# Exponentials of the routing on GpSimd instead of ScalarE, in twelve of sixteen row groups

## The chip, the cores and the metric

The kernel runs on one NeuronCore of a Trainium2 chip. TensorE (PE) multiplies matrices, VectorE (DVE) does elementwise work and reductions, ScalarE (ACT) evaluates functions, GpSimd (POOL) runs elementwise work in software and issues indirect DMAs, SyncE (SP) issues DMAs. Each engine takes its instructions in the order of the program and waits at semaphores. The metric is the device time of the launch in microseconds (us).

## The reference

```python
x = hidden_states                                  # (4, 2048, 256) fp32
x = x + _layernorm(attention(_layernorm(x)))       # "bump" attention, 16 heads
x = x + _layernorm(ffn(_layernorm(x)))
# attention, per head: out_i = sum_j max(0, 1 - |z_i - z_j| / b) * v_j / T
# ffn:
logits = x @ gate_w                                # 64 experts
probs = softmax(logits); w, idx = top_k(probs, 8)
w = w / sum(w)
y = sum over the 8 experts of w * expert(x)        # at most 128 rows per expert
shared = (silu(gu[:, :Is]) * gu[:, Is:]) @ shared_down_w * sigmoid(x @ shared_gate_w)
out = y + shared
```

## The kernel before, in words

The attention is computed by brute force. For each batch b (4 of them) and head, and for each of 16 blocks of 128 keys, one tile of 128 x 2048 holds the distances of the keys to all 2048 queries: 1024 tiles, 256 per batch. A tile passes through three engines. ScalarE writes |zq - zk| with an Abs activation (L1035); VectorE turns it in place into min(d, 1) - 1 (L1341); TensorE multiplies it with the values, in four column chunks (L859). For 87 "own" tiles VectorE makes the distances as well (L1365, then L1339); `own_tiles` chooses them beforehand from `WEIGHTS` and from the timetable. The tiles lie in a ring of NTB = 8 buffers: tile e may be written when tile e - 8 has been used by TensorE. `tensor_step(n)` (L844) multiplies chunk c of tile n - c, so that the last chunk of tile t is multiplied in step t + 3, which itself needs the finished tile t + 3.

All other work is threaded between these tiles by `timetable(b)`: each entry has a slot (0 to 255, a tile number within the batch) and a stage. During the tiles of batch b the rows of batch b - 1 go through the rest of the layer in four groups k of 512 rows. `rows_at(k)` = 8 + 12 k starts the first half (slots 4 to 60), `rest_at(k)` = 60 + 48 k the second, called r below. On VectorE a group runs: "xst" at r (statistics), "hn" at r + 5 and r + 6 (second layer norm), "lg" at r + 20 (logits), "rm" and "re" at r + 21 and r + 23 (the eight largest; the operands of the exponential, semaphore s_e), "sc" at r + 28, "sm" at r + 31 (sum of the eight exponentials and its reciprocal; 1/(1 + e^-g) for the shared gate), "gu" and "dn" between r + 24 and r + 49 (shared expert; "dn" multiplies with the gate). The next group has its "hn" at r + 53 and r + 54.

On ScalarE "ex" at r + 28 is the exponential over 128 x 260 elements: 64 shifted logits and one gate logit for each of 4 row tiles (L977). It stands between the Silu activations of "gu" (L993). A change between Exp and Silu makes the compiler put in an ACT_TABLE_LOAD.

GpSimd has no timetable, it works through a list: `pool_rstd` (L1494 to L1498) makes 1/sqrt(var + eps) for a group, from an addition and a power over 128 x 4 elements; "hn" waits for it. `pool_route` (L1500 to L1505) multiplies the exponentials with the mask of the eight chosen (s_w0, for which "sm" waits), and then with the reciprocal sum. At L1527 it subtracts 128 x 1024 elements, once for each of 12 groups. The fourth batch is the tail after the last tile (`scalar_tail`, `vector_tail`), where the same stages run without tiles.

Of the kernel before, what the change touches and what calls it, by code (L numbers as in the profile page):

```python
# [8 lines left out]
ALU = mybir.AluOpType  # L9
# [13 lines left out]


WEIGHTS = {"fst": 10, "fn": 7, "xT": 7, "v": 7, "z": 8, "zT": 3, "cst": 10, "cn": 7, "xst": 10, "hn": 7, "hT": 7, "lg": 4,
           "rm": 15, "re": 8, "sc": 14, "sm": 9, "gu": 7, "dn": 8}


def own_tiles():
# [42 lines left out]
def timetable(b):  # L72

    pe, dv, ac, sy = [], [], [], []
    if b:
        p = b - 1
        for k in range(4):
            r = rows_at(k)
            sy += [(r - 4, "a", p, k), (r + 13, "x1", p, k)]
            dv += [(r, "cst", p, k, 0), (r + 1, "cst", p, k, 1), (r + 5, "cn", p, k, 0), (r + 6, "cn", p, k, 1)]  # L80
            r = rest_at(k)
            sy += [(r - 2, "xl", p, k), (r + 9, "h", p, k), (r + 31, "cum", p, k), (r + 35, "w2", p, k), (r + 50, "y", p, k)]
            dv += [(r, "xst", p, k, 0), (r + 1, "xst", p, k, 1), (r + 5, "hn", p, k, 0), (r + 6, "hn", p, k, 1),
                   (r + 12, "hT", p, k), (r + 20, "lg", p, k), (r + 21, "rm", p, k), (r + 23, "re", p, k),
                   (r + 28, "sc", p, k), (r + 31, "sm", p, k)]
            ac += [(r + 15, "hT", p, k), (r + 28, "ex", p, k)]
            pe += [(r + 8, "hT", p, k, 0), (r + 9, "hT", p, k, 1), (r + 15, "lg", p, k, 0), (r + 16, "lg", p, k, 1),
                   (r + 24, "mT", p, k)]
            for m in range(4):
                for up in range(2):  # L90
                    pe += [(r + 17 + 6 * m + 3 * up, "gu", p, k, m, up)]
                ac += [(r + 23 + 6 * m, "gu", p, k, m)]
                dv += [(r + 24 + 6 * m, "gu", p, k, m)]
            for i in range(2):
                pe += [(r + 42 + 3 * i, "dn", p, k, i)]
                dv += [(r + 46 + 3 * i, "dn", p, k, i)]
# [148 lines left out]
def build(nc, x, Wq, bq, Wk, bk, WvT, bv, WpT, lbw, gates_w, sgu_w, sdn_w, egu_w, edn_w, out):  # L245
    with ExitStack() as ctx:
# [40 lines left out]
        qb = sb("qb", [128, 2])  # L287
        nzk = [sb(f"nzk{i}", [128, C]) for i in range(NB)]
        mhalf = sb("mhalf", [128, 4])
        st6 = [sb(f"st6{i}", [128, 4, 6]) for i in range(5)]  # L290
        mv = [sb(f"mv{i}", [128, 4, 2]) for i in range(5)]
        ve = [sb(f"ve{i}", [128, 4]) for i in range(5)]
# [36 lines left out]
        q_h = [sem(f"q_h{i}") for i in range(4)]  # L329
        q_zq, q_y, q_zy = sem("q_zq"), sem("q_y"), sem("q_zy")  # L330

        s_e, s_ex, s_w0, s_sm, s_wn = sem("s_e"), sem("s_ex"), sem("s_w0"), sem("s_sm"), sem("s_wn")
        q_cum = [sem(f"q_cum{i}") for i in range(4)]
        q_w2 = [sem(f"q_w2{i}") for i in range(4)]

# [766 lines left out]
        def vector_stage(v, what, b, k=0, i=0):  # L1102
# [116 lines left out]
            elif what == "sm":  # L1219
# [3 lines left out]
                dve.tensor_reduce(sm, R4, AX.X, ALU.add).then_inc(s_v, 1)  # L1223
                dve.wait_ge(s_v, v.up())
                dve.reciprocal(sm, sm).then_inc(s_sm, 1)
                dve.tensor_scalar(sg4, E4[:, :, 64], 1.0, None, ALU.add).then_inc(s_v, 1)
                dve.wait_ge(s_v, v.up())
                dve.reciprocal(sg[:, 4 * k:4 * k + 4], sg4).then_inc(s_v, 1)
# [172 lines left out]
        def vector_tail(v):  # L1401
# [21 lines left out]
            vector_stage(v, "sc", b, 3)  # L1423
            for k in range(4):
                vector_stage(v, "sm", b, k)
            vector_stage(v, "dn", b, 0, 0)
            vector_stage(v, "dn", b, 0, 1)
            dve.wait_ge(*tile_used(1023))
# [70 lines left out]

        def pool_route(b, k):  # L1500
            R4, M4, E4, mx, sm, sg4, cm = routing(b, k)
            pool.wait_ge(s_ex, 4 * b + k + 1)
            pool.tensor_tensor(R4, E4[:, :, 0:64], M4, ALU.mult).then_inc(s_w0, 1)  # L1503
            pool.wait_ge(s_sm, 4 * b + k + 1)
            pool.tensor_tensor(R4, R4, view(sm, 0, [[1, 4], [0, 64]]), ALU.mult).then_inc(s_wn, 1)  # L1505

        def pool_program():
# [4 lines left out]
            pool.affine_select(out=ident[:, :], in_=ident[:, :], compare_op=ALU.not_equal, fill=1.0, base=0,  # L1512
                               pattern=[[-1, 128]], channel_multiplier=1).then_inc(s_const, 1)
            pool.memset(mhalf[:, :], -0.5).then_inc(s_const, 1)
            pool.iota(scoli[:, :], pattern=[[0, 1]], base=0, channel_multiplier=1).then_inc(s_p, 1)
            pool.wait_ge(s_p, p.up())
            pool.tensor_copy(scol[:, :], scoli[:, :]).then_inc(s_const, 1)
            pool.wait_ge(s_const, 3)
            for k in range(4):
                pool_rstd(k, s_fmv, k + 1, s_frs, p)  # L1520
            for b in range(NB):
                if b:
                    for k in range(4):
                        pool_rstd(k, s_cmv, 4 * (b - 1) + k + 1, s_crs, p, 1e-5 * NT * NT)
                        pool.wait_ge(s_cn, 4 * (b - 1) + k + 1)
                        pool.wait_ge(q_a[k], 16 * b)
                        pool.tensor_tensor(x_of(b - 1, k), x_of(b - 1, k), ctxn[:, 4 * k:4 * k + 4, :],  # L1527
                                           ALU.subtract).then_inc(s_xs, 1)
                    for k in range(4):
                        pool_rstd(k, s_xmv, 4 * (b - 1) + k + 1, s_xrs, p)  # L1530
                        pool_route(b - 1, k)
                else:
                    for n in range(4, 4 * NB):
                        pool_rstd(n % 4, s_fmv, n + 1, s_frs, p)
# [14 lines left out]
            pool.memset(shift[:, 64:65], 0.0).then_inc(s_shift, 1)  # L1549
            for k in range(4):  # L1550
                pool_route(b, k)
            for k in range(4):
                pool.wait_ge(q_h[k], 64)
                pool.wait_ge(q_w2[k], 64)
# [82 lines left out]
```

## Time and profile before

| | |
|---|---|
| median of 3 runs | 2489.83 us (2488.68 to 2490.23) |
| profiled execution, its own time | 2490.41 us |
| its span, first to last instruction | 2489.1 us |
| busy: DVE, PE, ACT, POOL | 2022.5, 1964.6, 1958.0, 463.2 us |
| tiles run from about | 90 us to 2055 us |
| mean granted TensorE clock | 0.908 of 2.4 GHz |

"Busy" is the time in which an engine had an instruction in work; neighbouring instructions of one engine overlap a little. The span is 1.3 us shorter than the device time. A releaser ("<-") is the instruction whose semaphore ended a wait. In the timeline, consecutive instructions of one kind are merged: "x5" with 5.76 means five of them in 5.76 us.

### The profile page before, as it was taken

Reading aid. Unit: us, or ns where it says so; the run is one execution under the profiler, and the core shown is the slowest. Engines: PE = TensorE matmul, PEld = TensorE weight load, DVE = VectorE, ACT = ScalarE, POOL = GpSimd, SP = SyncE. Lnnn points to the kernel's source line nnn. Section 1 sums busy time; section 2 is a strip of 40 time slices with the busy share of each in tenths; the row PEclk is TensorE's granted clock in tenths of the full one; section 3 lists DMA queues with packets and bytes.
Section 4 is the critical chain, followed back from the end, with each engine's and each line's share of the span. In section 5 each row is a group of like instructions: output and inputs, shape, how many; then the busy total and the mean of one; then the engine's idle time right before and its main releaser. Section 6 shows DMA issues by size and latency. Waiting matters only on the chain.

```text
span 2489.1 us, 30196 instructions
## 1 busy us (share of the span) xinstructions
PE 1964.6 (79%) x11666; PEld 778.3 (31%) x11666; DVE 2022.5 (81%) x2896; ACT 1958.0 (79%) x1277; POOL 463.2 (19%) x331
## 2 busy tenths in 40 slices
PE   7788889788678888887788888768898884899920
PEld 4433233233113223221222322212332223577720
DVE  5497888887999898999898989999988986644349
ACT  2398998897999999999899999999999990122223
POOL 1010110100320000114010000141000001267754
PEclk9899999899989999998899999989999995798975
DMA  6315244335120202121202020312111107577779
GB/s 217 129 60 205 93 145 151 110 128 191 44 93 13 87 28 83 41 106 43 94 29 82 18 106 22 119 43 82 66 40 35 47 13 231 119 184 186 180 190 314
DMA packets 182039, 259.26 MB, mean 104 GB/s; under 512 B 22280, under 2 KB 162184, under 8 KB 173704
## 3 DMA queue, kind: packets, MB, share of 16 engines
q1 hardware_dynamic: 167408, 237.83, 28.7%
q0 software_dynamic: 12288, 18.88, 4.3%
q8 instruction: 94, 1.54, 0.3%
q10 hardware_dynamic: 2200, 0.60, 0.1%
q14 instruction: 49, 0.40, 0.1%
HBM read 187.25 MB, written 70.03 MB: 103 GB/s over the span
## 4 chain that ended last, share of the span: by engine, by line
ACT 36%; PE 33%; DVE 21%; issue 5%; DMA 3%; POOL 2%; SPq 1%; DVEq 0%; POOLq 0%; ACTq 0%
ACT TB L1035 33%; PE ps L859 10%; DVE TB L1341 8%; PE ps L765 5%; PE ps L803 4%; DVE TB L1365 4%; PE ps L810 3%; DVE st L1083 2%; PE ps L952 2%; DVE TB L1339 1%; PE ps L831 1%; POOL rs L1498 1%; PE ps L913 1%; PE ps L748 1%; PE ps L787 1%
## 5 line engine op out<-in xcount | busy, mean ns | idle before, releaser
L1035 ACT ACTIVATE TB<-ZB,nzk 128x2048 f32<-128x2048 f32 x937 | 1792.8, 1993 | 146.4 <-PE ps L859 99.9
L859 PE MATMUL ps<-TB,V 128*32 128x512 f32 x8192 | 1103.4, 638 | 301.3 <-DVE TB L1341 286.6
L1341 DVE TENSOR_SCALAR TB<-TB 128x2048 f32<-128x2048 f32 x937 | 1134.7, 1232 | 132.5 <-ACT TB L1035 128.6
L859 PEld LDWEIGHTS ps<-TB,V 128*32 128x32 f32 x8192 | 207.0, 112 | 1032.0 <-DVE TB L1341 657.8
L1496 POOL TENSOR_SCALAR ve<-mv 128x4 f32<-128x4 f32 x64 | 80.5, 1258 | 1215.5 <-DVE mv L1087 1215.5
L803 PE MATMUL ps<-XF,wsgu 128*128 128x512 f32 x512 | 265.0, 644 | 6.8 <-ACT XF L993 5.6
L1365 DVE SCALAR_TENSOR_TENSOR TB<-ZB,kz 128x2048 f32<-128x2048 f32 x87 | 214.8, 2469 | 4.3 <-PE ps L859 4.2
L1062 ACT ACTIVATE ZB<-ps 128x128 f32<-128x128 f32 x64 | 17.7, 277 | 186.4 <-PE ps L952 140.6
L803 PEld LDWEIGHTS ps<-XF,wsgu 128*128 128x128 f32 x512 | 94.0, 201 | 159.8 <-issue 140.2
L1339 DVE TENSOR_SCALAR TB<-TB,kz 128x2048 f32<-128x2048 f32 x87 | 122.7, 1410 | 0.0
L1498 POOL TENSOR_TENSOR rs<-ve,mhalf 128x4 f32<-128x4 f32 x64 | 113.8, 1778 | 5.3
L1503 POOL TENSOR_TENSOR scr<-scr 128x256 f32<-128x256 f32 x12 | 10.9, 912 | 539.7 <-ACT scr L977 539.7
L1594 POOL DMA_INDIRECT y_rows<-ZB x64 | 102.0, 1594 | 24.7 <-issue 15.8
L765 PE MATMUL ps<-scr,XF 128*128 128x512 f32 x192 | 100.1, 644 | 0.0
L810 PE MATMUL ps<-wsdn,XF 128*128 128x256 f32 x384 | 89.3, 386 | 0.0
L1463 DVE COPY ZB<-ps 128x256 f32<-128x256 f32 x64 | 27.0, 421 | 67.5 <-PE ps L942 49.1
L810 PEld LDWEIGHTS ps<-wsdn,XF 128*128 128x128 f32 x384 | 71.0, 190 | 28.8 <-issue 20.1
L822 PE MATMUL ps<-ident,cT 128*128 128x128 f32 x256 | 43.0, 293 | 42.3 <-DVE ctxn L1266 42.3
L1580 POOL DMA_INDIRECT TB<-h_rows,ZB x64 | 63.3, 989 | 64.4 <-ACT ZB L1069 31.9
L1258 DVE COPY cT<-ps 128x512 f32<-128x512 f32 x64 | 43.9, 686 | 35.4 <-PE ps L859 32.6
L765 PEld LDWEIGHTS ps<-scr,XF 128*128 128x128 f32 x192 | 53.0, 299 | 52.1 <-issue 39.5
L1527 POOL TENSOR_TENSOR scr<-scr,ctxn 128x1024 f32<-128x1024 f32 x12 | 61.0, 5086 | 43.5 <-DVE ctxn L1093 43.5
(176 smaller groups left out, 1606.0 us busy)
## 6 DMA issues: line engine op xcount, KB each, us to landing
ZB<-zq_rows SPq DMA_DIRECT2D x64, 1024.0 KB, 7.2
scr<-fused_w SPq DMA_DIRECT2D x48, 512.0 KB, 3.6
TB<-in_egu_w SPq DMA_DIRECT2D x44, 256.0 KB
y_rows<-zero SPq DMA_DIRECT2D x20, 512.0 KB, 4.9
fused_w<-TB SPq DMA_DIRECT2D x4, 2048.0 KB, 6.8
TB<-y_rows SPq DMA_DIRECT2D x16, 512.0 KB, 8.6
XF<-in_x SPq DMA_DIRECT2D x24, 256.0 KB, 3.2
v_rows<-scr SPq DMA_DIRECT2D x24, 256.0 KB, 2.2
```

What stands on the lines that cost most here:

```text
L765: ins = pe.matmul(ps[bank][:, :], view(X0, NT * c + tt, [[16, 128]]), w[:, c, :], start=(tt == 0 and c == 0), stop=(tt == 15 and c == 1))
L803: ins = pe.matmul(ps[bank][:, :], wsgu[:, c, o:o + 128], hT_of(b, k)[:, c, :], start=(c == 0), stop=(c == 1))
L810: ins = pe.matmul(ps[bank][:, 256 * t:256 * t + 256], act_of(b)[:, mm, 128 * (2 * i + t):128 * (2 * i + t) + 128], wsdn[:, mm, :], start=( ...
L859: ins = pe.matmul(ps[c][32 * j:32 * j + 32, :], V[:, o:o + 32], tile(t)[:, 512 * c:512 * c + 512], start=(kb == 0), stop=(kb == KB - 1))
L1035: act.activation(tile(e), zrow(head), ACT.Abs, bias=nzk[b][:, kb * H + g:kb * H + g + 1], scale=1.0).then_inc(s_abs, 1)
L1339: dve.tensor_scalar(T, T, top, top, ALU.min, ALU.subtract).then_inc(s_bump, 1)
L1341: dve.tensor_scalar(T, T, 1.0, 1.0, ALU.min, ALU.subtract).then_inc(s_bump, 1)
L1365: dve.scalar_tensor_tensor(tile(e), zrow(head), kz[:, 0, kb * H + g:kb * H + g + 1], zrow(head), ALU.subtract, ALU.max, reverse0=True).the ...
L1496: pool.tensor_scalar(ve[s][:, :], view(mv[s][:, 0, 1:2], 0, [[2, 4]]), eps, None, ALU.add).then_inc(s_p, 1)
L1498: pool.tensor_tensor(rs[s][:, :], ve[s][:, :], mhalf[:, 0:4], ALU.pow).then_inc(done, 1)
L1580: pool.indirect_dma_start(xe[s], None, XH, bass.IndirectOffsetOnAxis(ap=idx2[:, order[n]:order[n] + 1].bitcast(u32), axis=0)).then_inc(q_x ...
L1594: pool.indirect_dma_start(Y[c], bass.IndirectOffsetOnAxis(ap=idx2[:, order[n]:order[n] + 1].bitcast(u32), axis=0), ye[n % NX], None, compu ...
```

## The change

For the twelve groups of the first three batches the exponential leaves ScalarE. GpSimd computes it as a power: a tensor with the constant e (`ebase`, read with a stride of 0) raised to the operand. The gate's column (128 x 4) comes first with a semaphore of its own, then the other 256 columns. The stage "sm" is split: "sg" (the gate's 1/(1 + e^-g), weight 4) stands at r + 40 and "sm" (the sum, weight 5) at r + 54, which is 31 tiles behind "re". The DMA of the weights ("w2") goes from r + 35 to r + 58. In GpSimd's list the multiplication with the reciprocal sum of a group moves behind the `pool_rstd` of the next one. The four groups of the tail keep ScalarE's exponential.

```diff
-           "rm": 15, "re": 8, "sc": 14, "sm": 9, "gu": 7, "dn": 8}
+           "rm": 15, "re": 8, "sc": 14, "sm": 5, "sg": 4, "gu": 7, "dn": 8}
...
-            sy += [(r - 2, "xl", p, k), (r + 9, "h", p, k), (r + 31, "cum", p, k), (r + 35, "w2", p, k), (r + 50, "y", p, k)]
+            sy += [(r - 2, "xl", p, k), (r + 9, "h", p, k), (r + 31, "cum", p, k), (r + 58, "w2", p, k), (r + 50, "y", p, k)]
...
-                   (r + 28, "sc", p, k), (r + 31, "sm", p, k)]
-            ac += [(r + 15, "hT", p, k), (r + 28, "ex", p, k)]
+                   (r + 28, "sc", p, k), (r + 40, "sg", p, k), (r + 54, "sm", p, k)]
+            ac += [(r + 15, "hT", p, k)]
...
+        ebase = sb("ebase", [128, 1])
...
+            elif what == "sg":
+                R4, M4, E4, mx, sm, sg4, cm = routing(b, k)
+                if b == last:
+                    dve.wait_ge(s_ex, 4 * b + k + 1)
+                else:
+                    dve.wait_ge(s_eg, 4 * b + k + 1)
                 dve.tensor_scalar(sg4, E4[:, :, 64], 1.0, None, ALU.add).then_inc(s_v, 1)
...
         def pool_route(b, k):
             R4, M4, E4, mx, sm, sg4, cm = routing(b, k)
+            if b != last:
+                pool.wait_ge(s_e, 4 * b + k + 1)
+                pool.tensor_tensor(E4[:, :, 64:65], view(ebase[:, 0:1], 0, [[0, 4], [0, 1]]), E4[:, :, 64:65],
+                                   ALU.pow).then_inc(s_eg, 1)
+                pool.tensor_tensor(E4[:, :, 0:64], view(ebase[:, 0:1], 0, [[0, 4], [0, 64]]), E4[:, :, 0:64],
+                                   ALU.pow).then_inc(s_ex, 1)
             pool.wait_ge(s_ex, 4 * b + k + 1)
             pool.tensor_tensor(R4, E4[:, :, 0:64], M4, ALU.mult).then_inc(s_w0, 1)
+
+        def pool_weights(b, k):
+            R4, M4, E4, mx, sm, sg4, cm = routing(b, k)
             pool.wait_ge(s_sm, 4 * b + k + 1)
             pool.tensor_tensor(R4, R4, view(sm, 0, [[1, 4], [0, 64]]), ALU.mult).then_inc(s_wn, 1)
...
+            pool.memset(ebase[:, :], 2.718281828459045).then_inc(s_const, 1)
...
                     for k in range(4):
                         pool_rstd(k, s_xmv, 4 * (b - 1) + k + 1, s_xrs, p)
+                        if k:
+                            pool_weights(b - 1, k - 1)
                         pool_route(b - 1, k)
+                    pool_weights(b - 1, 3)
```

GpSimd's list, from the statistics of the first batch's second group (k = 1) to those of the third. Before, one multiplication waits for ScalarE (s_ex) and one for VectorE (s_sm):

```order
L1496 TENSOR_SCALAR ve<-mv 128x4 [waits s_xmv]
L1498 TENSOR_TENSOR rs<-ve,mhalf 128x4 [waits s_p]
L1503 TENSOR_TENSOR scr<-scr 128x256 [waits s_ex]
L1505 TENSOR_TENSOR scr<-scr 128x256 [waits s_sm]
L1496 TENSOR_SCALAR ve<-mv 128x4 [waits s_xmv]
```

Now two powers (L1512, L1514) stand ahead of the first multiplication (L1517), and the next group's L1504 and L1506, for which VectorE's "hn" waits, stand behind all three:

```order
L1504 TENSOR_SCALAR ve<-mv 128x4 [waits s_xmv]
L1506 TENSOR_TENSOR rs<-ve,mhalf 128x4 [waits s_p]
L1522 TENSOR_TENSOR scr<-scr 128x256 [waits s_sm]
L1512 TENSOR_TENSOR scr<-ebase,scr 128x4 [waits s_e]
L1514 TENSOR_TENSOR scr<-ebase,scr 128x4x64
L1517 TENSOR_TENSOR scr<-scr 128x256 [waits s_ex]
L1504 TENSOR_SCALAR ve<-mv 128x4 [waits s_xmv]
```

The multiplication by the reciprocal sum (L1505, now L1522) has moved behind the next group's `pool_rstd`; the L1522 shown here belongs to group k = 0.

ScalarE, around the exponential of one group. Before, a table load, the exponential, one Abs tile and a second table load (the group's second Silu follows):

```order
L993 ACTIVATE XF<-ps 128x512 [waits full5,full6]
L1035 ACTIVATE TB<-ZB,nzk 128x2048 [waits s_used] x4
L977 ACT_TABLE_LOAD
L977 ACTIVATE scr<-scr 128x260 [waits s_e]
L1035 ACTIVATE TB<-ZB,nzk 128x2048 [waits s_used]
L993 ACT_TABLE_LOAD
L993 ACTIVATE XF<-ps 128x512 [waits full5]
```

Now the same four Abs tiles and the one behind the exponential run on without a break to that second Silu:

```order
L994 ACTIVATE XF<-ps 128x512 [waits full5,full6]
L1036 ACTIVATE TB<-ZB,nzk 128x2048 [waits s_used] x5
L994 ACTIVATE XF<-ps 128x512 [waits full5]
```

VectorE, around the second layer norm (L1094) of the second group, in the changed kernel. The tile instruction is L1348 (L1341 before):

```order
L1348 TENSOR_SCALAR TB<-TB 128x2048 [waits s_abs] x4
L1094 TENSOR_SCALAR scr<-scr,mv,rs 128x256 [waits q_y,s_xrs]
L1094 TENSOR_SCALAR scr<-scr,mv,rs 128x256
L1348 TENSOR_SCALAR TB<-TB 128x2048 [waits s_abs]
L1224 TENSOR_REDUCE scr<-scr 128x4 [waits s_ex,s_w0]
L1226 RECIPROCAL scr<-scr 128x4 [waits s_v]
```

The sum (L1224; L1223 before) stood before directly ahead of the gate's two instructions, six instructions behind the scan of "sc"; now it stands behind the first half of the next group's "hn". `own_tiles` gives 86 own tiles instead of 87.

## Rows read from the trace of the kernel before

**Rows 1.** The page, busy time, share of the span, instructions.

```profile
PE 1964.6 (79%) x11666; PEld 778.3 (31%) x11666; DVE 2022.5 (81%) x2896; ACT 1958.0 (79%) x1277; POOL 463.2 (19%) x331
```

**Rows 2.** Stretches: length, then busy time and count of PE, PEld, DVE, ACT, POOL, clock.

```profile
620.00:720.00 100.00, 68.32 (x460) 12.14 (x452) 97.15 (x115) 93.71 (x50) 34.72 (x12) 0.87 0.15 50
812.00:905.00 93.00, 78.22 (x504) 26.10 (x500) 81.87 (x103) 89.70 (x53) 4.80 (x4) 0.98 0.19 66
```

**Rows 3.** Waits in 812:905: who waited for whom, us in total, times, longest.

```profile
DVE TB L1341 <- ACT TB L1035: 8.8, 12, 1.2
ACT TB L1035 <- PE ps L859: 3.8, 4, 1.5
```

**Rows 4.** Groups of ACT: op, shapes, count, busy us, mean ns, idle before.

```profile
L993 ACT ACT_TABLE_LOAD x13 | 16.7, 1283 | 0.2
L977 ACT ACT_TABLE_LOAD x13 | 16.7, 1283 | 0.2
...
L977 ACT ACTIVATE scr<-scr 128x260 f32<-128x260 f32 x12 | 5.0, 420 | 0.1
```

**Rows 5.** Timeline of ACT: start us, us, engine, line, op.

```profile
903.42 24.73 ACT L1035 ACTIVATE TB<-ZB,nzk 128x2048 f32<-128x2048 f32 x13 [0.97 <-PE ps L859]
...
946.05 3.89 ACT L1035 ACTIVATE TB<-ZB,nzk 128x2048 f32<-128x2048 f32 x2
949.96 1.28 ACT L977 ACT_TABLE_LOAD   x1
951.25 0.42 ACT L977 ACTIVATE scr<-scr 128x260 f32<-128x260 f32 x1
```

**Rows 6.** Timeline of POOL in the tail, and the group of the second multiplication there.

```profile
2063.64 0.23 POOL L1496 TENSOR_SCALAR ve<-mv 128x4 f32<-128x4 f32 x1 [48.01 <-DVE mv L1087]
2063.96 1.04 POOL L1498 TENSOR_TENSOR rs<-ve,mhalf 128x4 f32<-128x4 f32 x1
...
L1505 POOL TENSOR_TENSOR TB<-TB 128x256 f32<-128x256 f32 x4 | 2.4, 612 | 5.1 <-DVE TB L1225 5.1
```

**Rows 7.** Lines L1341, L1365 of DVE: duration ns min/median/max.

```profile
L1341 DVE TENSOR_SCALAR TB<-TB x937: 1191/1219/3399, 93.6 to 2050.1; 128x2048 f32<-128x2048 f32 x188
...
L1365 DVE SCALAR_TENSOR_TENSOR TB<-ZB,kz x87: 2336/2344/4467, 115.7 to 2034.3; 128x2048 f32<-128x2048 f32 x87
```

**Rows 8.** Timelines of DVE and of POOL, 655:664.

```profile
656.86 2.35 DVE L1341 TENSOR_SCALAR TB<-TB 128x2048 f32<-128x2048 f32 x2
659.13 4.46 DVE L1365 SCALAR_TENSOR_TENSOR TB<-ZB,kz 128x2048 f32<-128x2048 f32 x1
...
657.02 4.42 POOL L1527 TENSOR_TENSOR scr<-scr,ctxn 128x1024 f32<-128x1024 f32 x1 [2.63 <-DVE ctxn L1093]
```

**Rows 9.** Timelines of DVE and of POOL around 774.

```profile
774.29 1.71 DVE L1341 TENSOR_SCALAR TB<-TB 128x2048 f32<-128x2048 f32 x1
...
773.13 1.78 POOL L1503 TENSOR_TENSOR scr<-scr 128x256 f32<-128x256 f32 x1 [46.44 <-ACT scr L977]
```

**Rows 10.** Timelines of DVE and of POOL, 997:1004.

```profile
997.12 3.46 DVE L1341 TENSOR_SCALAR TB<-TB 128x2048 f32<-128x2048 f32 x3
1000.77 1.23 DVE L1341 TENSOR_SCALAR TB<-TB 128x2048 f32<-128x2048 f32 x1 [0.18 <-ACT TB L1035]
...
999.57 2.46 POOL L1498 TENSOR_TENSOR rs<-ve,mhalf 128x4 f32<-128x4 f32 x1
```

**Rows 11.** Timelines: operands ready, next group's rstd and "hn", 853 to 911.

```profile
853.05 0.42 DVE L1208 TENSOR_TENSOR scr<-scr 128x256 f32<-128x256 f32 x1
...
910.55 0.74 DVE L1093 TENSOR_SCALAR scr<-scr,mv,rs 128x256 f32<-128x256 f32 x2
...
905.82 2.20 POOL L1496 TENSOR_SCALAR ve<-mv 128x4 f32<-128x4 f32 x1 [34.62 <-DVE mv L1087]
908.10 2.42 POOL L1498 TENSOR_TENSOR rs<-ve,mhalf 128x4 f32<-128x4 f32 x1
```

**Rows 12.** Timeline of PE: the matmuls of one tile.

```profile
1391.36 1.06 PE L859 MATMUL ps<-TB,V 128*32 128x512 f32 x8 [0.82 <-DVE TB L1341]
```

More of the change, by code:

```diff
@@ L330, in build @@
         q_zq, q_y, q_zy = sem("q_zq"), sem("q_y"), sem("q_zy")
-        s_e, s_ex, s_w0, s_sm, s_wn = sem("s_e"), sem("s_ex"), sem("s_w0"), sem("s_sm"), sem("s_wn")
+        s_e, s_eg, s_ex, s_w0, s_sm, s_wn = sem("s_e"), sem("s_eg"), sem("s_ex"), sem("s_w0"), sem("s_sm"), sem("s_wn")
         q_cum = [sem(f"q_cum{i}") for i in range(4)]
@@ L1425, in vector_tail @@
                 vector_stage(v, "sm", b, k)
+                vector_stage(v, "sg", b, k)
             vector_stage(v, "dn", b, 0, 0)
@@ L1517, in pool_program @@
             pool.tensor_copy(scol[:, :], scoli[:, :]).then_inc(s_const, 1)
-            pool.wait_ge(s_const, 3)
+            pool.wait_ge(s_const, 4)
             for k in range(4):
@@ L1551, in pool_program @@
                 pool_route(b, k)
+                pool_weights(b, k)
             for k in range(4):
```

## Prediction

> **What bounds the kernel now.** I read the page's busy times first: three engines lie within 60 us of each other [rows 1], so an average decides nothing. The busy time by stretches does. While a group of rows goes through "rest" (812 to 905 us, 48 tiles), ACT is busy 89.7 us of 93, VectorE 81.9, PE 78.2 [rows 2]. The waits of the same stretch agree: VectorE's tile instruction waits 8.8 us for ACT's, ACT only 3.8 us for PE [rows 3]. Where the first half of the rows goes through (620 to 720 us), VectorE is busy 97.2 us of 100 [rows 2]; the change takes nothing out there. So ACT bounds the twelve stretches in which the exponentials stand, and what leaves ACT there shortens the kernel nearly one for one, as long as VectorE keeps delivering. A tile costs ACT 24.73/13 = 1.90 us from start to start [rows 5], VectorE some 1.15 us (2.35 for two [rows 8]) and PE 1.06 us [rows 12].
>
> **What ACT gains.** Per group one exponential of 0.42 us and two table loads of 1.283 us go [rows 4]; in the order the Exp load and the Silu load behind it are both gone. That is 2.99 us, of which some 0.1 us lay over the next instruction, so 2.9 us, and for twelve groups 35 us. The tail's pair stays. One own tile less gives ACT one Abs more (1.9 us), so 33 us. The waits left in rows 3 say that ACT would get most of it.
>
> The Trainium skill puts a higher price on a change of table (ScalarE: Activation LUTs, "What ACT_TABLE_LOAD costs": about 1.28 us for the load and 1.38 us of draining, 2.66 us together). The trace does not show the drain as added time: two Abs that start at 946.05 take 3.89 us and end at 949.94, the load starts at 949.96 and the exponential at 951.25 [rows 5]. By the page the gain would be 24 x 1.38 = 33 us larger; I go by the rows.
>
> **What VectorE gains and loses in instructions.** Nothing: "sg" and "sm" are the old four instructions in two places, with one own tile less. SP's "w2" goes behind "y"; rows that wait for it ("rm" of the next group, 11 slots later) have 20 us. The 512-byte constant and its memset are before the loop.
>
> **What GpSimd now has to do.** No row shows a power over 256 elements. The nearest are the power over 128 x 4 in a quiet place, 1.04 us, the addition over 128 x 4 beside it, 0.23 us, and a multiplication over 128 x 256, 0.61 us [rows 6]. The lower bound is that multiplication, 0.6 us. If all of the small power's time grows with the columns, it is 256 x 1.04/4 = 66.6 us. I take off what an instruction costs anyway: (1.04 - 0.23)/4 = 0.20 us for one column, 256 x 0.2025 + 0.23 = 52 us. It may be less, if part of the 0.81 us is a preparation done once; with half of it so, 26 us. I take 52 us: a column is the unit in which GpSimd works on all partitions, and the multiplication's 0.61 us shows a preparation of at most a few tenths.
>
> **What that does to VectorE.** This is where the sum turns. GpSimd and VectorE show a collision in the trace of before. L1527 (128 x 1024) starts at 657.02 and ends at 661.44; VectorE's L1365 starts at 659.13 and takes 4.46 us instead of 2.34, so that it ends 2.15 us behind GpSimd's end, its whole own work [rows 7, 8]. GpSimd first waited for VectorE's instructions to end, then had the memory to itself, and VectorE stood. The same happened in all twelve L1527: each has one VectorE tile instruction beside it that is longer by up to 2.2 us (L1341 up to 3399 ns against 1219 [rows 7]). The multiplication over 256 columns did it too: L1503 ends at 774.91, the L1341 that started at 774.29 ends at 776.00, 1.09 us later [rows 9]. So for the time in which GpSimd streams through its operands, VectorE's tile instruction does not move.
>
> The four-column power is different: 999.57 to 1002.03, and in its middle an L1341 runs from 1000.77 in its ordinary 1.23 us [rows 10]. Four columns are fetched at once, the computing (some 0.9 us) holds nothing up, and the result waits for the end of VectorE's instruction. With 256 columns, one consumed each 0.2 us, the fetching lasts as long as the computing, unless GpSimd can take in a large share of them beforehand or lets go of the memory between columns. I take it that it holds on. Then VectorE stands for about 50 of the 52 us, twelve times.
>
> The Trainium skill says it more strictly (SBUF — State Buffer, "SBUF: two separate sides"): the port pair that the two engines share is an exclusive lock which the one that starts first keeps for the whole instruction, while the other is blocked. Rows 8 and 9 agree; rows 10 do not, as the small power did not keep it while it computed. By the page the hold is the full 52 us; by rows 10 the last few columns' worth less.
>
> **What the hold costs.** ACT can go on while VectorE stands, until the ring is full. With tile d waiting for VectorE, PE has finished step d - 1 and freed tile d - 4, so ACT may write up to d + 4: four tiles, 4 x 1.90 = 7.6 us. Afterwards VectorE (1.15) and PE (1.06) have to pass one tile before ACT goes on, 2.2 us. ACT loses 52 - 7.6 + 2.2 = 46.6 us per group. As ACT is the bound, nothing gives that back: 12 x 46.6 = 559 us. PE, idle for 45 us, may come back at the lower clock; the stretches of before with much idle PE had 0.87 [rows 2], and PE has room, so I add nothing.
>
> **The sum.** The profiled execution took 2490.4 us, 0.6 above the median. 2490.4 - 33 + 559 = 3016; I say 3010 us for the median. This mechanism's own range goes from 2740 (a power of 30 us: 12 x 24.6 = 295, less 33) to 3110 (60 us: 12 x 54.6 = 655, less 33); with 66.6 us it would be 3190.
>
> **Rivals.**
> *GpSimd lets go of the memory between columns (faster).* The power runs beside the tiles, and the layout of the change fits. Speaking for it: rows 10, where computing held nothing. Against it: in rows 8 GpSimd, once it had the memory, kept it for 1024 columns while VectorE was asking. What is late next is the next group's "hn", since `pool_rstd` stands behind the power in GpSimd's list. From the operands (853.47) to "hn" (910.55) there are 57.1 us [rows 11], 54 when ACT is faster. GpSimd needs some 2.4 for the gate, 52, 0.7, and 2.2 + 2.4 for rstd [rows 11], together 59.7: 5.7 us late, of which the ring covers 5.4. Gain 33 less 3 to 6: 2461 us (2455 to 2475). This decides as soon as VectorE's tile instructions keep 1.2 us during a power.
> *No hold, but a power of 60 us or more (slower).* "hn" waits in VectorE's order and all tiles behind it. At 60 us it is 13.7 us late, 8.3 beyond the ring, 12 x 8.3 = 100 less 33: 2557 us. It turns from gain to loss at about 54.5 us; at 66.6 us 2636. For it speaks only the upper bound.
> *A short power (0.6 to 10 us).* Most of the 1.04 us would be preparation. Held or not, at most 12 x (10 - 5.4) = 55 us against 33: 2457 to 2512, around no change at 8 us. Speaking against it is that it needs 0.8 us before the first column.
>
> **Chances.** Hold with a long power 0.60; no hold and a gain 0.27; no hold and the wait for "hn" 0.06; short power 0.07, half of it within 0.2%. A measurement of this kernel tells 0.2%, 5 us, from no change. Faster 0.30, same 0.05, slower 0.65. The range that holds 8 in 10 must reach the gain: 2455 to 3090; below lie some 0.05, above some 0.12.
>
> **What would show it.** If I am right, L1514's twelve instructions last about 52 us and in each of them one tile instruction of VectorE (L1348, L1346 or L1372) lasts about 50 us, with ACT idle some 40 us on PE and the GpSimd's busy time up by some 600 us; ACT's table loads are down by 24. Mis-sized but right: the same with another length. Wrong: L1348 keeps its maximum of 3.4 us; then the time is below 2480 if "hn" does not wait for GpSimd, and the first place to look is the idle time before L1094 with the releaser L1506.

## The result, and the profile after

The changed kernel took **2452.86 us** (median of 4, 2448.18 to 2456.26) against 2490.03 us (median of 4, 2488.68 to 2493.73) for the kernel before: ratio of the executions 0.9847, 95% interval 0.9829 to 0.9865. That is 37 us faster, where 3010 us, 520 slower, was forecast. It is the outcome of the first rival, "GpSimd lets go of the memory between columns", whose sum was 2461 us (2455 to 2475); its mechanism came out differently, as the experiments show. The profiled execution of after took 2456.26 us, span 2455.0 us, mean granted clock 0.906 of 2.4 GHz. All rows of after below are from it.

Busy times, as in [rows 1]:

```profile
PE 1961.3 (80%) x11666; PEld 779.4 (32%) x11666; DVE 2015.5 (82%) x2895; ACT 1923.6 (78%) x1242; POOL 999.9 (41%) x356
```

GpSimd's busy time is up by 537 us, where some 600 were foreseen, but VectorE's has fallen by 7 us, although busy time includes the time in which an instruction is held up (the small program below shows one of 163.9 us). ACT has 34 us and 35 instructions less: 24 table loads, 12 exponentials, and one Abs more.

The two powers (groups of GpSimd: busy us, mean ns, idle before):

```profile
L1514 POOL TENSOR_TENSOR scr<-ebase,scr 128x256 f32<-128x256 f32 x12 | 509.7, 42471 | 0.0
L1512 POOL TENSOR_TENSOR scr<-ebase,scr 128x4 f32<-128x4 f32 x12 | 29.4, 2452 | 388.1 <-DVE scr L1209 388.1
```

The lines of VectorE that answer to [rows 7], with minimum, median and maximum in ns:

```profile
L1348 DVE TENSOR_SCALAR TB<-TB x938: 1191/1218/3404, 93.7 to 2013.0; 128x2048 f32<-128x2048 f32 x188
L1372 DVE SCALAR_TENSOR_TENSOR TB<-ZB,kz x86: 2336/2344/4467, 115.6 to 1997.2; 128x2048 f32<-128x2048 f32 x86
```

The power takes 42 us where 52 were forecast. The sign of a hold would have been twelve tile instructions of about 50 us. The maxima are those of before, to 5 ns; of L1346, which also works on tiles, to 6 ns (3397 against 3391).

One power on GpSimd (start us, us), and the tile instructions of VectorE that lie inside it:

```profile
761.51 1.93 POOL L1512 TENSOR_TENSOR scr<-ebase,scr 128x4 f32<-128x4 f32 x1 [34.93 <-DVE scr L1209]
763.40 42.31 POOL L1514 TENSOR_TENSOR scr<-ebase,scr 128x256 f32<-128x256 f32 x1
805.80 0.68 POOL L1517 TENSOR_TENSOR scr<-scr 128x256 f32<-128x256 f32 x1
809.38 2.20 POOL L1504 TENSOR_SCALAR ve<-mv 128x4 f32<-128x4 f32 x1 [2.90 <-DVE mv L1088]
...
763.67 1.43 DVE L1348 TENSOR_SCALAR TB<-TB 128x2048 f32<-128x2048 f32 x1 [0.51 <-ACT TB L1036]
765.57 1.23 DVE L1348 TENSOR_SCALAR TB<-TB 128x2048 f32<-128x2048 f32 x1 [0.47 <-ACT TB L1036]
```

The tile that starts right behind the power's start is 0.2 us longer than the median, the next one is ordinary. GpSimd is through with everything at 806.48 and then itself waits 2.9 us for the next group's statistics; in the nine groups that have a next one it is 1.0 to 8.4 us. No wait of the second layer norm ("hn") for GpSimd is in the trace. All that the sums wait for is this, once, in the last group of a batch:

```profile
1075.94 0.42 DVE L1224 TENSOR_REDUCE scr<-scr 128x4 f32<-128x256 f32 x1 [1.05 <-POOL scr L1517]
```

Busy times by stretches, the first two as in [rows 2], the third inside one power (ACT and POOL are the fourth and fifth pair):

```profile
620.00:720.00 100.00, 68.10 (x460) 12.17 (x452) 97.13 (x115) 93.72 (x50) 34.74 (x12) 0.87 0.15 50
810.00:899.00 89.00, 76.18 (x492) 25.32 (x492) 81.33 (x104) 87.81 (x51) 50.75 (x7) 1.00 0.20 68
765.00:805.00 40.00, 36.22 (x219) 12.63 (x218) 37.58 (x36) 40.00 (x25) 40.00 (x1) 1.00 0.06 17
```

With the power under way ACT is busy without a gap and PE 36.2 us of 40 at the full 2.4 GHz. The first stretch, where VectorE is the limit, is unchanged. The waits of the second, as in [rows 3]:

```profile
DVE TB L1348 <- ACT TB L1036: 6.3, 11, 1.1
ACT TB L1036 <- PE ps L860: 1.1, 2, 0.8
```

VectorE still waits more for ACT than ACT for PE: ACT is still the bound here, and the time of the kernel fell by about what left ACT.

### The profile page after: what moved, and what is told of

Read it like the earlier page. It is cut to its first block, busy times and chain, and to the rows that moved or that the text cites. A ratio compares the mean times of both kernels' runs of the same rounds, so it can differ in the third digit from the quotient of the medians.

```text
span 2455.0 us, 30185 instructions
## 1 busy us (share of the span) xinstructions
PE 1961.3 (80%) x11666; PEld 779.4 (32%) x11666; DVE 2015.5 (82%) x2895; ACT 1923.6 (78%) x1242; POOL 999.9 (41%) x356
## 4 chain that ended last, share of the span: by engine, by line
PE 35%; ACT 28%; DVE 24%; POOL 5%; issue 4%; DMA 3%; SPq 1%; DVEq 0%; POOLq 0%; ACTq 0%
ACT TB L1036 28%; PE ps L860 11%; DVE TB L1348 9%; PE ps L766 5%; PE ps L804 4%; DVE TB L1372 4%; PE ps L811 3%; DVE st L1084 2%; PE ps L953 2%; POOL scr L1514 2%; DVE TB L1346 2%; POOL rs L1506 1%; POOL ve L1504 1%; PE ps L914 1%; PE ps L832 1%
## 5 line engine op out<-in xcount | busy, mean ns | idle before, releaser
L1036 ACT ACTIVATE TB<-ZB,nzk 128x2048 f32<-128x2048 f32 x938 | 1794.7, 1994 | 144.4 <-PE ps L860 97.6
L1348 DVE TENSOR_SCALAR TB<-TB 128x2048 f32<-128x2048 f32 x938 | 1129.0, 1228 | 101.0 <-ACT TB L1036 98.9
L1514 POOL TENSOR_TENSOR scr<-ebase,scr 128x256 f32<-128x256 f32 x12 | 509.7, 42471 | 0.0
L1504 POOL TENSOR_SCALAR ve<-mv 128x4 f32<-128x4 f32 x64 | 84.1, 1314 | 837.0 <-DVE mv L1088 837.0
L804 PE MATMUL ps<-XF,wsgu 128*128 128x512 f32 x512 | 259.1, 631 | 1.1 <-DVE TB L1255 0.6
L1512 POOL TENSOR_TENSOR scr<-ebase,scr 128x4 f32<-128x4 f32 x12 | 29.4, 2452 | 388.1 <-DVE scr L1209 388.1
L1346 DVE TENSOR_SCALAR TB<-TB,kz 128x2048 f32<-128x2048 f32 x86 | 121.4, 1411 | 0.0
L1506 POOL TENSOR_TENSOR rs<-ve,mhalf 128x4 f32<-128x4 f32 x64 | 114.8, 1793 | 5.3
L1545 POOL TENSOR_TENSOR scr<-scr,ctxn 128x1024 f32<-128x1024 f32 x12 | 61.0, 5080 | 36.0 <-DVE ctxn L1094 36.0
```

Source lines behind the costliest of these rows:

```text
L804: ins = pe.matmul(ps[bank][:, :], wsgu[:, c, o:o + 128], hT_of(b, k)[:, c, :], start=(c == 0), stop=(c == 1))
L1036: act.activation(tile(e), zrow(head), ACT.Abs, bias=nzk[b][:, kb * H + g:kb * H + g + 1], scale=1.0).then_inc(s_abs, 1)
L1346: dve.tensor_scalar(T, T, top, top, ALU.min, ALU.subtract).then_inc(s_bump, 1)
L1348: dve.tensor_scalar(T, T, 1.0, 1.0, ALU.min, ALU.subtract).then_inc(s_bump, 1)
L1504: pool.tensor_scalar(ve[s][:, :], view(mv[s][:, 0, 1:2], 0, [[2, 4]]), eps, None, ALU.add).then_inc(s_p, 1)
L1506: pool.tensor_tensor(rs[s][:, :], ve[s][:, :], mhalf[:, 0:4], ALU.pow).then_inc(done, 1)
```

## Experiments

Three are small programs of their own that compute nothing of the layer (the output is a copy of the input). In them GpSimd does powers and products of several widths, while VectorE repeats the kernel's tile instruction (128 x 2048, in place) beside a short reduction.

**The power alone and beside VectorE.** GpSimd does one instruction with n = 4, 16, 64, 256, 1024, first with VectorE idle, then beside pairs of tile instruction and reduction, then beside 60 tile instructions without a gap, last beside one VectorE instruction over 128 x 16384.

```diff
+        pool.tensor_tensor(F[:, 0:n], view(base[:, 0:1], 0, [[0, n]]), E[:, 0:n], ALU.pow)
+        dve.tensor_scalar(t, t, 1.0, 1.0, ALU.min, ALU.subtract)   # t: 128 x 2048
+        dve.tensor_reduce(red[:, :], sm[:, :], AX.X, ALU.add)
```

> A small program of its own, nothing of the layer: GpSimd runs powers over 4, 16, 64, 256 and 1024 columns and multiplications over 256 and 1024, first alone, then beside pairs of VectorE instructions (a 128x2048 tile instruction and a 128x256 reduction), then powers beside tile instructions without gaps, then a power over 64 and 256 columns and a multiplication over 1024 columns that each meet one VectorE instruction over 16384 columns (about 9.1 us). Theory A (GpSimd fetches a few columns ahead at VectorE's gaps and lets go again): alone 256 columns take the 42 us of the changed kernel, beside the pairs within 1 us of it, with tile instructions at 1.2 us; beside the 9.1 us instruction the power over 256 is longer by 5 to 8 us. Theory B (all operands are fetched at the start): the same beside the pairs, one tile instruction longer by 0.2 to 0.5 us at the start, and no lengthening by the 9.1 us instruction; over 1024 columns either the hold at the start grows to 1 to 2 us or columns beyond the store are fetched later. Theory C (GpSimd keeps the memory after all, and what let VectorE run in the changed kernel is something else): tile instructions of some 10, 40 or 160 us beside the powers over 64, 256 and 1024. The multiplications hold VectorE for 0.6 and 2.2 us under each theory.

GpSimd: alone (36 to 255 us), beside pairs (276 and 318), in the gapless chain (703), beside the long instruction (822):

```profile
35.77 1.04 POOL L78 TENSOR_TENSOR F<-base,E 128x4 f32<-128x4 f32 x1
39.87 10.52 POOL L80 TENSOR_TENSOR F<-base,E 128x64 f32<-128x64 f32 x1
50.47 41.13 POOL L81 TENSOR_TENSOR F<-base,E 128x256 f32<-128x256 f32 x1
91.67 163.21 POOL L82 TENSOR_TENSOR F<-base,E 128x1024 f32<-128x1024 f32 x1
...
276.30 42.27 POOL L97 TENSOR_TENSOR F<-base,E 128x256 f32<-128x256 f32 x1
318.65 164.20 POOL L98 TENSOR_TENSOR F<-base,E 128x1024 f32<-128x1024 f32 x1
703.47 66.64 POOL L108 TENSOR_TENSOR F<-base,E 128x4 f32<-128x4 f32 x1 [214.56 <-DVE TB L56]
822.32 41.12 POOL L128 TENSOR_TENSOR F<-base,E 128x256 f32<-128x256 f32 x1
```

VectorE at the same times:

```profile
277.56 1.30 DVE L56 TENSOR_SCALAR TB<-TB 128x2048 f32<-128x2048 f32 x1
...
320.04 163.90 DVE L56 TENSOR_SCALAR TB<-TB 128x2048 f32<-128x2048 f32 x1
...
823.97 8.68 DVE L134 TENSOR_SCALAR BIG<-BIG 128x16384 f32<-128x16384 f32 x1
```

With 256 columns the tile instruction inside the power is 0.1 us longer, as theory B has it. An 8.68 us VectorE instruction that runs inside the power neither holds it up (41.12 us) nor is held up, which rules out theory A: the columns that were due until it ended, an estimated 60 at 0.16 us each, were already in. That the other columns were in as well follows less directly, from the pairs: inside the power only the first tile instruction is longer than 1.21 us. With 1024 columns one tile instruction stands 163.9 us, 1.1 us past the power's end, as only theory C had it. So the forecast's hold exists, but not at this change's width. The power's time is (41.13 - 10.52)/192 = 0.16 us for a column and some 0.4 us besides, and beside VectorE it is at most 1.2 us longer than alone.

**Without the large power.** Left out: the exponential of the 256 columns.

```diff
-                pool.tensor_tensor(E4[:, :, 0:64], view(ebase[:, 0:1], 0, [[0, 4], [0, 64]]), E4[:, :, 0:64],
-                                   ALU.pow).then_inc(s_ex, 1)
```

> The changed kernel without the power over 256 columns (the exponentials of the experts are left out, the weights come out wrong; the gate's column is kept). If the power costs VectorE and the tiles nothing (theory A or B): 2448 to 2456 us, as the changed kernel. If the power costs something beside the tiles (a fetch held at each gap of VectorE, 12 x 256 columns at some ns each): 5 to 30 us faster than the changed kernel.

2455.06 us (2449.63 to 2458.05), ratio to before 0.9865 (0.9845 to 0.9884), after 0.9847. Taking out 510 us of GpSimd's work changes nothing: the two intervals leave room for some 6 us in all, against 559 forecast.

**The moves alone.** After's order and waits, the exponential on ScalarE, no powers.

```diff
-            ac += [(r + 15, "hT", p, k)]
+            ac += [(r + 15, "hT", p, k), (r + 28, "ex", p, k)]
```

> The order of the changed kernel (sum and weights late, weights behind the next group's rstd), but with the exponential on ScalarE and no power on GpSimd. If the gain is ScalarE's freed time: 2485 to 2495 us, as before the change. If the gain comes from the moves on VectorE, SP and GpSimd: 2450 to 2460 us.

2485.67 us, ratio 0.9978 (0.9958 to 0.9997). The moves bring some 0.2%, at most 0.4%; some 33 of the 37 us are ScalarE's, give or take 7. (`own_tiles` gives 87 own tiles here, as before, since the exponentials stand in ScalarE's timetable again.)

**The exponential on ScalarE and a power beside it.** As the last, and GpSimd raises e to the 256 columns of the mask, as a load whose result is overwritten.

```diff
+                pool.tensor_tensor(R4, view(ebase[:, 0:1], 0, [[0, 4], [0, 64]]), M4, ALU.pow).then_inc(s_eg, 1)
```

> As the moves alone, with ScalarE's exponential, and a power over 256 columns on GpSimd beside it that raises e to the mask into the buffer that the multiplication then overwrites: the power's cost by itself. Theory A or B: within 3 us of the moves alone. Theory C or a cost at each fetch: slower than the moves alone by 5 us or more.

2488.88 us, ratio 0.9993 (0.9979 to 1.0006), 3 us above the kernel without the power. The two intervals overlap, so that the 3 us are not clear of noise.

**The sums early.** "sg" and "sm" at r + 31, so that VectorE waits for the power. It tells what the ring of buffers gives back after a stall.

```diff
-                   (r + 28, "sc", p, k), (r + 40, "sg", p, k), (r + 54, "sm", p, k)]
+                   (r + 28, "sc", p, k), (r + 31, "sg", p, k), (r + 31, "sm", p, k)]
```

> The changed kernel with the gate's and the sum's VectorE instructions back at r + 31, 8 tiles behind the operands; the powers stay on GpSimd. The sum then waits in VectorE's order for the power: operands to end of the multiplication 44.7 us, 8 tiles are 15 us, so 29.7 us late. With the ring's run-ahead of four tiles (5.4 us of it regained) 24.3 x 12 = 292 us: 2745 us. If the ring regains nothing: 356 us, 2809 us. If the wait stays hidden: 2453 us.

2818.82 us (2815.84 to 2821.79), ratio 1.1324 (1.1263 to 1.1385): 366 us over after, for this wait of VectorE:

```profile
DVE scr L1224 <- POOL scr L1517: 353.1, 12, 34.1
```

The ring gave nothing back (2809 us were expected for that case). Why is seen at one stall, on DVE, ACT and PE:

```profile
805.89 0.42 DVE L1224 TENSOR_REDUCE scr<-scr 128x4 f32<-128x256 f32 x1 [28.29 <-POOL scr L1517]
806.46 2.35 DVE L1372 SCALAR_TENSOR_TENSOR TB<-ZB,kz 128x2048 f32<-128x2048 f32 x1
...
774.06 9.57 ACT L1036 ACTIVATE TB<-ZB,nzk 128x2048 f32<-128x2048 f32 x5
783.52 0.59 ACT L994 ACTIVATE XF<-ps 128x512 f32<-128x512 f32 x1
811.95 2.00 ACT L1036 ACTIVATE TB<-ZB,nzk 128x2048 f32<-128x2048 f32 x1 [27.85 <-PE ps L860]
815.94 3.90 ACT L1036 ACTIVATE TB<-ZB,nzk 128x2048 f32<-128x2048 f32 x2 [1.98 <-PE ps L860]
820.57 3.90 ACT L1036 ACTIVATE TB<-ZB,nzk 128x2048 f32<-128x2048 f32 x2 [0.73 <-PE ps L860]
...
810.00 1.94 PE L860 MATMUL ps<-TB,V 128*32 128x512 f32 x8 [31.46 <-DVE TB L1348]
```

VectorE stood from 777.6 to 805.9. ACT worked on until 784.1, 6.5 us longer, near the forecast's 7.6. But it started again 6.1 us after VectorE, not 2.2: VectorE had an own tile's distances to make first (2.35 us), and PE took 1.94 us for a tile instead of 1.06 [rows 12]. In the stretch 810 to 814 us its granted clock was 0.50, the level of 1.2 GHz, after 28 us with almost nothing to do; from 814 to 820 us it was 0.99 again. Then ACT waited 2.7 us more.

**The power twice.** A second, useless power over 256 columns behind the first; it delays `pool_rstd`.

```diff
+                pool.tensor_tensor(R4[:, :, 0:64], view(ebase[:, 0:1], 0, [[0, 4], [0, 64]]), M4[:, :, 0:64],
+                                   ALU.pow).then_inc(s_xx, 1)
+                pool.wait_ge(s_xx, 4 * b + k + 1)
```

> The changed kernel with a second power over 256 columns behind the first (of the mask, into the buffer that the multiplication overwrites). No hold and a wait of the next group's second layer norm: rstd is done 90.6 us behind the operands, VectorE comes at 52.9, so 37.7 us late, less 5.4 is 32.3, nine times 291 us; in the three last groups of a batch the sum is late by 39, less 5.4, 101 us: 2845 us. If the ring regains nothing: 2453 + 9 x 37.7 + 3 x 39 = 2909 us. If the hold exists at 256 columns: tile instructions of 40 us in the trace.

2859.04 us (2857.37 to 2860.71), ratio 1.1486 (1.1425 to 1.1546), 406 us over after for 419 us of waits of VectorE (and no tile instruction above 4.5 us, so no hold here either):

```profile
DVE scr L1095 <- POOL rs L1507: 303.1, 9, 34.8
DVE scr L1225 <- POOL scr L1521: 116.2, 3, 41.8
```

**A quarter more.** The same with 64 columns, 10.5 us of GpSimd for each group.

```diff
-                pool.tensor_tensor(R4[:, :, 0:64], view(ebase[:, 0:1], 0, [[0, 4], [0, 64]]), M4[:, :, 0:64],
+                pool.tensor_tensor(R4[:, :, 0:16], view(ebase[:, 0:1], 0, [[0, 4], [0, 16]]), M4[:, :, 0:16],
```

> The changed kernel with a second power over 64 columns only (10.4 us) behind the first. The three layer norms of a batch are then 7.5, 7.1 and 3.5 us late, the last group's sum 11.4 us. With the ring's 5.4 us regained: 3 x (2.1 + 1.7 + 0 + 6.0) = 29 us, 2482 us. With nothing regained: 3 x 29.5 = 88 us, 2541 us.

2488.76 us, ratio 1.0000 (0.9976 to 1.0025). The same two waits are 29.9 us (9 times, 4.2 at most) and 24.8 us (3 times, 11.5 at most); together 54.7 us. The profiled execution, the fastest of the ten, is 24 us above after's; by the medians 36 us reach the end, between the two expectations. So a power of 52 us, the forecast's length, would have used up the gain even without a hold, within the 6 us of the interval. The reserve is uneven: in after "hn" follows the operands by 52.1 to 57.5 us in the nine groups (52.9 in the first, 761.4 to 814.3), where I had 54 for all, and the sum of a batch's last group, which waits up to 11.5 us here, was not in my sum.

**One power.** The gate's column and the 256 others in one instruction of 260; "sg" waits for it.

```diff
-                pool.tensor_tensor(E4[:, :, 64:65], view(ebase[:, 0:1], 0, [[0, 4], [0, 1]]), E4[:, :, 64:65],
-                                   ALU.pow).then_inc(s_eg, 1)
-                pool.tensor_tensor(E4[:, :, 0:64], view(ebase[:, 0:1], 0, [[0, 4], [0, 64]]), E4[:, :, 0:64],
-                                   ALU.pow).then_inc(s_ex, 1)
+                pool.tensor_tensor(E4, view(ebase[:, 0:1], 0, [[0, 4], [0, 65]]), E4, ALU.pow).then_inc(s_ex, 1)
```

> The changed kernel with one power over all 260 columns instead of the gate's column first. The gate's VectorE instructions at r + 40 come 31.5 us behind the operands and wait until 43, so 11.5 us, twelve times 138 us. Long waits (the early sum) cost their whole length: 2591 us; waits of the size of the quarter more cost two thirds: 2543 us. If the gate's own instruction is worth nothing: 2453 us.

2631.0 us (2624.35 to 2635.94), ratio 1.0544 (1.0522 to 1.0566): 178 us over after, more than both expectations and more than VectorE's waits for the power, the first row; ACT's waits for PE, the second, were 97.6 us in after:

```profile
DVE scr L1230 <- POOL scr L1509: 143.0, 12, 14.0
ACT TB L1036 <- PE ps L860: 270.0, 106, 13.0
```

One of the gate's waits shows why more is lost than VectorE waits. Behind the 12.4 us for which VectorE stood, PE needed 3.64 us for two tiles, against 1.92 ahead of it, and ACT waited three times:

```profile
805.40 3.64 PE L860 MATMUL ps<-TB,V 128*32 128x512 f32 x16 [11.67 <-DVE TB L1345]
...
807.36 3.90 ACT L1036 ACTIVATE TB<-ZB,nzk 128x2048 f32<-128x2048 f32 x2 [10.81 <-PE ps L860]
```

With the two waits behind it (2.63 and 0.57 us) ACT lost 14.0 us there. The granted clock was 1.00 from 778 to 792 us and 0.50, the level of 1.2 GHz, from 805 to 809. Twelve such losses, an estimate from this one, are 168 of the 178 us. That the gate's column goes first is worth 178 us. Without it the change is a loss.

**Widths.** The first small program with other widths beside pairs, and products and sums for comparison.

```diff
+        step(pool.tensor_tensor(F[:, 0:512], bcast(512), E[:, 0:512], ALU.pow))
+        step(pool.tensor_tensor(F[:, 0:768], bcast(768), E[:, 0:768], ALU.pow))
+        step(pool.tensor_tensor(F[:, 0:512], G[:, 0:512], E[:, 0:512], ALU.pow))
```

> The small program again, to find the width from which GpSimd holds VectorE. Beside pairs of VectorE instructions (tile instruction and reduction) GpSimd runs powers over 256, 288, 320, 384, 512 and 768 columns with the base as one repeated column, powers over 256 and 512 columns with two full operands, multiplications over 64 to 1024 columns and additions with one input over 256, 512 and 1024. Theory B with a store of limited size (fetching runs ahead of the computing by some hundred columns; the memory is held from the first fetch to the last): up to the store's width a tile instruction is longer by 0.1 to 0.4 us; beyond it, it is longer by the time in which the rest is consumed: for a store of 256 columns (768 - 256) x 0.16 = 82 us at 768 and 41 us at 512. Theory D (beyond a width the memory is held from start to end, as the 164 us at 1024 columns suggest): nothing up to the width, and the whole 82 and 123 us at 512 and 768. Multiplications: held for their time less what is stored, so the 256 holds 0.2 us and the 1024 some 1.8 us.

The powers over 512 and 768 columns and the product over 1024:

```profile
366.16 83.86 POOL L90 TENSOR_TENSOR F<-base,E 128x512 f32<-128x512 f32 x1
450.09 123.47 POOL L91 TENSOR_TENSOR F<-base,E 128x768 f32<-128x768 f32 x1
...
714.82 2.34 POOL L102 TENSOR_TENSOR F<-G,E 128x1024 f32<-128x1024 f32 x1
```

The tile instructions beside the powers over 256, 512 and 768 columns, and beside the product (1.21 us undisturbed):

```profile
160.39 1.53 DVE L56 TENSOR_SCALAR TB<-TB 128x2048 f32<-128x2048 f32 x1
367.44 1.73 DVE L56 TENSOR_SCALAR TB<-TB 128x2048 f32<-128x2048 f32 x1
451.34 123.31 DVE L56 TENSOR_SCALAR TB<-TB 128x2048 f32<-128x2048 f32 x1
714.95 3.29 DVE L56 TENSOR_SCALAR TB<-TB 128x2048 f32<-128x2048 f32 x1
```

Up to 512 columns the tile instruction loses 0.1 to 0.5 us, though the powers last up to 84 us; at 768 it stands for the whole power, not for the part above a limit (theory D). Two full operands instead of a constant make little difference (1.42 and 1.95 us beside 256 and 512 columns). Products over 128, 256, 512 and 1024 columns stretch it to 1.40, 1.67, 2.21 and 3.29 us, by about 0.2 us for 100 columns; additions with one input over 256, 512 and 1024 columns stretch it less, to 1.35, 1.57 and 1.99 us.

**Widths near the limit.** The same with 528, 576, 640, and 768 as two halves of 384.

```diff
+        step(pool.tensor_tensor(F[:, 0:528], bcast(528), E[:, 0:528], ALU.pow))
+        step(pool.tensor_tensor(F[:, 0:576], bcast(576), E[:, 0:576], ALU.pow))
+        step(pool.tensor_tensor(F[:, 0:384], bcast(384), E[:, 0:384], ALU.pow))
```

> The small program, beside pairs of VectorE instructions: powers over 528, 576 and 640 columns with a repeated base, one over 640 with two full operands, and two over 384 columns in place of one over 768. If GpSimd's store takes in 512 columns and everything wider is held throughout: one tile instruction of 85, 93 and 103 us at 528, 576 and 640, and none above 1.6 us for the two halves. If the limit lies higher (640 to 767): no long tile instruction here up to it.

VectorE's held instructions: two at 528 columns (the power runs from 37.04 to 122.71), then 576 (93.05 us long), and the first half of 384 (63.04):

```profile
37.21 1.98 DVE L56 TENSOR_SCALAR TB<-TB 128x2048 f32<-128x2048 f32 x1
119.81 3.99 DVE L56 TENSOR_SCALAR TB<-TB 128x2048 f32<-128x2048 f32 x1
124.04 92.88 DVE L56 TENSOR_SCALAR TB<-TB 128x2048 f32<-128x2048 f32 x1
...
423.92 1.52 DVE L56 TENSOR_SCALAR TB<-TB 128x2048 f32<-128x2048 f32 x1
```

The limit lies between 512 and 528 columns. At 528 only the last 2.8 us are held, from 576 the whole power (at 640 columns 103.0 of 103.2 us). Two halves hold 0.3 us each.

**The subtraction on VectorE.** After's one large collision left is L1545 (L1527 before), 128 x 1024 on GpSimd, which costs VectorE up to 2.2 us [rows 7, 8] where VectorE is the limit. It goes to VectorE, whose "cn" stage has the code for the tail.

```diff
-                if b == last and i:
+                if i:
                     dve.wait_ge(s_cn, 4 * b + k + 1)
...
-                        pool.tensor_tensor(x_of(b - 1, k), x_of(b - 1, k), ctxn[:, 4 * k:4 * k + 4, :],
-                                           ALU.subtract).then_inc(s_xs, 1)
```

> The changed kernel with the subtraction over 128x1024 (twelve times) on VectorE instead of GpSimd. GpSimd's held one VectorE tile instruction for 2.1 us each time; on VectorE it takes 1.23 us (the tail's rows). In that stretch VectorE is busy 97 of 100 us, so 12 x 0.9 = 11 us less: 2442 us. If VectorE is not the bound there, or its new wait for the load of x costs as much: 2453 us or more.

**2438.37 us** (2435.9 to 2445.32), ratio to before 0.9782 (0.9763 to 0.9802), 14.5 us below after and the fastest of all. Lines of VectorE (as [rows 7]), and below them the stretch where the first halves run (as [rows 2]):

```profile
L1157 DVE TENSOR_TENSOR scr<-scr,ctxn x12: 1224/1226/1226, 631.2 to 1626.5; 128x1024 f32<-128x1024 f32 x12
L1348 DVE TENSOR_SCALAR TB<-TB x938: 1192/1222/1643, 92.2 to 1996.8; 128x2048 f32<-128x2048 f32 x188
```

```profile
620.00:720.00 100.00, 69.62 (x479) 12.09 (x472) 97.76 (x126) 98.65 (x53) 23.53 (x10) 0.88 0.20 68
```

Twelve instructions of 1.23 us are added and VectorE's busy time still falls by 8 us (2007.7), so that each of the twelve collisions had cost it about 1.9 us. The longest tile instruction falls from 3.40 to 1.64 us, and in these 100 us ACT does 98.7 us of work instead of 93.7.

**And more own tiles.** As the last, with 98 own tiles instead of 86, since ACT was still the bound in "rest".

```diff
-            ahead += 7 - beside[n] - (11 if q and 1 <= i < 7 else 0)
+            ahead += 7.5 - beside[n] - (11 if q and 1 <= i < 7 else 0)
```

> As the subtraction on VectorE, with 98 own tiles instead of 86 (7.5 instead of 7 in the rule). Each own tile takes 1.9 us from ScalarE and gives VectorE 2.6 us; where ScalarE is busy 88 of 89 us and VectorE 81, some 9 of them gain up to 1.5 us each, where VectorE is the bound 3 or 4 lose 2.6: 2435 us, between 2425 and 2450.

2443.78 us (2439.34 to 2444.72), ratio 0.9795 (0.9778 to 0.9811): inside the expected range, but no gain. Over the whole span VectorE's waits for ACT fall from 93.1 to 80.7 us and ACT's for PE rise from 83.5 to 106.7 us. The wait moved to another pair of engines; why was not examined further.

## Why the prediction was wrong

**What bounds the kernel: right.** ACT in the twelve "rest" stretches, VectorE in the first halves. 33 us taken from ACT came out as some 33 us of time (moves alone against after), 37 with the moves.

**ACT's gain without the drain: right.** Forecast 33 us; with the drain of 1.38 us that the Trainium skill (ScalarE: Activation LUTs, "What ACT_TABLE_LOAD costs") puts beside each load it would have been an estimated 66. The runs give 33 to 37, about 1.28 us for each load and the exponentials; here the measurement decides against the drain.

**The power's length: mis-sized.** Forecast 52 us, measured 42. The small power's 1.04 us in [rows 6] holds four columns of 0.16 us and about 0.4 us fixed; I had taken the addition's 0.23 us as all that is fixed. The quarter more shows that these 10 us decided between the gain and none.

**"I take it that it holds on": the step that failed.** I read [rows 8] as "for the time in which GpSimd streams through its operands" and then set fetching and computing equal. The first half is right. The second is not: the power over 256 columns takes its operands in at the start, for some 0.2 us of VectorE's time, and then computes without the memory, as far as the small programs show it. [Rows 10] showed just that with four columns, and I named the condition under which it would go on ("unless GpSimd can take in a large share of them beforehand") but gave it no width of its own to be tested by. L1527 (128 x 1024) is no counter-example: a product over 256, 512 and 1024 columns holds VectorE 0.5, 1.0 and 2.1 us in the small program, that is in proportion to what is fetched. [Rows 9] said the same for 256 columns: there the tile instruction took 1.71 us against 1.22, a hold of 0.5 us, which was the right upper estimate of what the change's fetch could cost. The 1.09 us that I read there is what VectorE still had to do behind GpSimd's end, not the hold. The hold, 559 us of the sum, came out as 0 (no large power: 2455.06; with it 2452.86).

The rule of the Trainium skill (SBUF — State Buffer, "SBUF: two separate sides") that the lock is exclusive and kept for the whole instruction fits the products here, and the powers from 576 columns up; at this change's width the measurement decides against it. With 576 columns or more the forecast's sum would have been the right one in kind, going by the small programs; no such width was run in the kernel.

**The ring's 5.4 us: wrong.** I subtracted what ACT can write ahead and added one tile's passage. The sums placed early show that the restart costs as much as was gained: 353 us of waits cost 366. For short waits some of it comes back (55 us cost 24 to 36), for the gate's wait more than all is lost (143 cost 178). I had also added nothing for PE's clock: behind the two stalls looked at it was at 0.50, and PE took 1.8 to 1.9 times as long for a tile.

**The rival's wait of "hn": did not occur,** for the reason above: with 42 us instead of 52 GpSimd is done 1.0 to 8.4 us before the next statistics. Hence 2453 instead of 2461. That the two lie so near is luck: at 52 us the wait would have cost some 24 to 36 us (the quarter more), not the 3 to 6 of that sum. The sum also counted twelve waits, and only nine groups have a next one. Nor does GpSimd let go between columns, as that rival had it: it needs the memory at the start only.

**Slips in the sums.** The lower end of the mechanism's own range is 2490 - 33 + 295 = 2752 us, not 2740. The three busiest engines lie within 65 us, not 60. Neither changes the argument.

**The chances.** 0.60 on the hold rested on one row of 1024 columns against one of 4; neither was near 256. No row spoke more for the one than for the other. The measured 2452.86 us lie 2 us below the lower end of the stated range, 2455.

**Left open.** Why at 528 columns the hold comes at the end and from 576 at the start. Whether the limit counts columns or bytes: only 4-byte elements were run.

## What to carry to other kernels

Ask of a GpSimd instruction beside VectorE not how long it takes but how long it fetches: here a slow function of 42 us over 256 columns was free in the kernel, and one of 84 us over 512 cost a tile instruction 0.5 us in the small program, while a cheap subtraction over 1024 columns cost VectorE about 2 us each, and moving those to VectorE gained 14.5 us. A long wait set into an in-order engine cost its full length in spite of a ring of eight buffers (353 us cost 366), so give each value its own semaphore (the gate's column: 178 us), and measure the reserve as well: here 10 us more per group on GpSimd ate the whole gain.

## What the runs showed of the hardware

- GpSimd's power with a 4-byte base and exponent: 0.16 us per column of 128 partitions, alone or (up to 2 us more in all) beside VectorE, with a constant or a full first operand.
- The hold of a power jumps from 0.5 us at 512 columns to the whole instruction at 576.
- The other direction is as hard: tile instructions of VectorE without a gap kept a 4-column power, 1.04 us alone, in work for 66.6 us, to the end of the chain. In the kernel it shows too: a power over 256 columns that ran beside four gapless tile instructions took 45.8 us instead of 42.

```profile
1029.34 45.80 POOL L1514 TENSOR_TENSOR scr<-ebase,scr 128x256 f32<-128x256 f32 x1
...
1029.01 4.62 DVE L1348 TENSOR_SCALAR TB<-TB 128x2048 f32<-128x2048 f32 x4
```
